# First attention: the transfers of the maximum rows issued by ACT instead of SyncE

## The reference: what is computed

```python
qkv = (x @ Wqkv).reshape(B, T, 3, H, D).transpose(2, 0, 3, 1, 4)    # 16 heads of 8
q, k, v = rope(qkv[0]), rope(qkv[1]), qkv[2]
att = einsum('bhqd,bhkd->bhqk', q, k) * scale
att = softmax(where(causal, att, -inf), axis=-1)
out = einsum('bhqk,bhkd->bhqd', att, v).transpose(0, 2, 1, 3).reshape(B, T, C)
x = layernorm(x + out @ Wo + bo)
```

## Time and profile before

| | |
|---|---|
| median of 3 runs | 1115.69 us (1115.14 to 1118.65) |
| profiled execution | 1117.81 us, of which 1116.1 us are the span from the first to the last instruction |
| busy: PE, DVE, ACT, POOL | 65%, 56%, 48%, 44% of the span |
| exps of the first attention, L2370 | 96 of 1023 ns |
| reduces of the first attention, L2319 and L2322 | 96 of 1223 ns |
| transfers of a load, L2136 | 192, median 0.68 to 0.69 us to issue |
| transfers of maximum rows, L2144 | 64 of 6 KB, median 0.70 us to issue |

### The profile page before, as it was taken

How to read it: one execution, slowest core, us unless ns; L and a number is a source line. 1 busy time by engine, 2 the same in 40 slices (tenths; PEclk the granted TensorE clock), 3 DMA queues, 4 the chain that set the end, 5 groups by cost and what they waited for, 6 DMA issues and landing times. The chain is left out here.

```text
span 1116.1 us, 20000 instructions
## 1 busy us (share of the span) xinstructions
PE 727.9 (65%) x6532; PEld 411.1 (37%) x6532; DVE 624.4 (56%) x1502; ACT 530.7 (48%) x849; POOL 491.0 (44%) x594
## 2 busy tenths in 40 slices
PE   3822578888847899999768499999681112386700
PEld 1411244444423344444233256556370111254500
DVE  2943468677556877777766223233477789321214
ACT  1420456666625666666457477777421006422102
POOL 0871346555542455555336444444208100468831
PEclk8965689999969999999989699999855555599955
DMA  7533322222000000000036899888006200144454
GB/s 156 177 118 90 108 67 69 66 73 71 6 1 1 0 1 1 1 1 1 1 113 213 204 186 181 150 155 155 2 0 193 75 1 1 27 89 91 60 116 124
DMA packets 138476, 87.72 MB, mean 79 GB/s; under 512 B 10722, under 2 KB 134050, under 8 KB 138274
## 3 DMA queue, kind: packets, MB, share of 16 engines
q1 hardware_dynamic: 132770, 82.57, 30.7%
q0 software_dynamic: 5632, 4.20, 2.8%
HBM read 56.99 MB, written 29.36 MB: 77 GB/s over the span
## 5 line engine op out<-in xcount | busy, mean ns | idle before, releaser
L1211 POOL TENSOR_TENSOR m_prod<-m_upc,m_gatec 128x512 f32<-128x512 f32 x64 | 99.6, 1557 | 114.7 <-DVE m_upc L1063 114.7
L2370 ACT ACTIVATE a_prob<-a_ps_pair 128x1024 f32<-128x1024 f32 x96 | 96.5, 1023 | 59.8 <-PE a_ps_pair L2181 56.8
L2411 POOL TENSOR_SCALAR_AFFINE_SELECT a_prob<-a_prob 128x512 f32<-128x512 f32 (+1 forms) x96 | 75.5, 787 | 105.7 <-ACT a_prob L2370 105.1
L2319 DVE TENSOR_REDUCE a_mx<-a_ps_pair 128x4 f32<-128x1024 f32 x64 | 78.0, 1223 | 77.6 <-PE a_ps_pair L2222 77.5
L751 POOL TENSOR_SCALAR_AFFINE_SELECT a_prob<-a_prob 128x512 f32<-128x512 f32 (+1 forms) x96 | 75.5, 787 | 97.3 <-ACT a_prob L713 97.3
L713 ACT ACTIVATE a_prob<-a_ps_b 128x1024 f32<-128x1024 f32 x96 | 98.6, 1029 | 31.2 <-PE a_ps_b L448 29.5
L1798 POOL DMA_INDIRECT m_y<-normed,m_idx x32 | 31.0, 970 | 103.2 <-DVE m_idx L1886 93.7
L1153 ACT ACTIVATE m_gate<-m_ps_g,bgu 128x512 f32<-128x512 f32 x64 | 43.9, 686 | 53.5 <-PE m_ps_g L914 53.4
L937 PE MATMUL m_ps_d<-m_act,wd 128*128 128x512 f32 x128 | 65.6, 594 | 2.3 <-DVE m_act L1073 2.3
L914 PE MATMUL m_ps_g<-m_x1T,wgu 128*128 128x512 f32 x128 | 65.8, 596 | 0.0
L916 PE MATMUL m_ps_u<-m_x1T,wgu 128*128 128x512 f32 x128 | 65.4, 592 | 0.0
(11 more groups left out here) (281 smaller groups left out, 1818.2 us busy)
## 6 DMA issues: line engine op xcount, KB each, us to landing
scratch_q<-p_parts SPq DMA_DIRECT2D x16, 384.0 KB, 2.6
scratch_k<-p_parts SPq DMA_DIRECT2D x16, 384.0 KB, 2.6
qst<-scratch_q SPq DMA_DIRECT2D x32, 192.0 KB, 3.3
kst<-scratch_k SPq DMA_DIRECT2D x32, 192.0 KB, 4.0
w<-in_w SPq DMA_DIRECT2D x8, 578.0 KB
qst<-scratch_q SPq DMA_DIRECT2D x64, 64.0 KB, 3.5
kst<-scratch_k SPq DMA_DIRECT2D x64, 64.0 KB, 4.0
qst<-scratch_q SPq DMA_DIRECT2D x32, 128.0 KB, 3.4
```

What stands on the lines that cost most here:

```text
L1211: nc.gpsimd.tensor_tensor(prod[:, n % 2, :], upc[:, n % 2, :], gatec[:, n % 2, :], ALU.mult).then_inc(s_pr, 1)
L2319: nc.vector.reduce_max(mx[:, w % 2, :, 2 * f:2 * f + 2, 1:2], pair[p][:, :].rearrange("p (m h k) -> p m h k", m=2, h=2), AX_X).then_inc(s_ ...
L2370: nc.scalar.activation(prob[:, r % 6, :], pair[(0, 2, 1)[j]][:, :], ACT.Exp, scale=scale, bias=0.0).then_inc(s_e, 1)
L2411: nc.gpsimd.affine_select(out=blk, in_=blk, compare_op=ALU.is_ge, fill=0.0, base=0, pattern=[[0, n], [1, P]], channel_multiplier=-1).then_ ...
```

## The change

The two transfers of maximum rows of a slot move from SP's program to ACT's. They stand at the end of ACT's turn, behind `exp(u, 2)`, and wait for the same copy as before. `copy_max` gets a wait until the transfers that read the same place of `mT` two slots earlier have landed. SP keeps the loads and the later weights; its loop starts at u = 0.

```diff
-                def max_rows(w):
-                    sp.wait_ge(s_mTc, w + 1)
-                    for m in range(2):
-                        r0 = 64 * m + max_row
-                        sp.dma_start(qst[r0:r0 + 3, w % BUFS, :, :].rearrange("p h (x q) -> p (h x) q", q=P),
-                                     mT[24 * m:24 * m + 24, w % 2, :]).then_inc(s_mrow[w % 2], 16)
...
-                for u in range(1 - LEAD, NU):
-                    if u + 2 < NU:
-                        max_rows(u + 2)
-                    if u % 2 == 1 and 0 <= u and u + BUFS < NU:
+                for u in range(NU):
+                    if u % 2 == 1 and u + BUFS < NU:
                         load((u - 1 + BUFS) // 2)
...
                 def copy_max(w):
                     act.wait_ge(s_mT, w + 1)
+                    after(act, s_mrow[w % 2], 32 * (w // 2))
                     nc.scalar.activation(mT[:, w % 2, :], ps_y[0:48, 0:64].bitcast(BF16), ACT.Copy).then_inc(s_mTc, 1)
+
+                def max_rows(w):
+                    act.wait_ge(s_mTc, w + 1)
+                    for m in range(2):
+                        r0 = 64 * m + max_row
+                        act.dma_start(qst[r0:r0 + 3, w % BUFS, :, :].rearrange("p h (x q) -> p (h x) q", q=P),
+                                      mT[24 * m:24 * m + 24, w % 2, :]).then_inc(s_mrow[w % 2], 16)
...
                     if 0 <= u < NU:
                         exp(u, 2)
+                    if 0 <= u + 2 < NU:
+                        max_rows(u + 2)
```

## The result

The changed kernel takes 1080.34 us (median of 4 runs, 1078.48 to 1081.46) against 1117.17 for the kernel before, run beside it (1115.14 to 1120.32). The ratio is 0.9666, with a 95% interval of 0.9637 to 0.9696: 36.8 us less, where 38.2 were predicted. The profiled execution took 1080.62 us with a span of 1078.9. In the changed file the lines stand a little higher: L2171 is the first scores matmuls (L2181 before), L2195 the fill that needs the stacks (L2205), L2360 the exps (L2370), L2365 the copy of the maxima (L2374), and L2372 is the new issue on ACT. L2309 and L2312 are the reduces, L2242 the transposed maxima, L2412 the mask and L2420 to L2426 `split_max`, the four small steps in which POOL splits the maxima.

A forecast was written before the change was run, and what follows sets the result against it. SP's issuing of transfers was taken to bound the first attention; 24.0 us up to slot 6 plus 14.2 us after it, with ACT's share nothing, made 38.2 us less: 1077.5 us, range 1070 to 1100 (1070 to 1084 without rivals).

The forecast's parts named there:

- The start: First attention, slot 0: ACT issues the rows behind its copy; PE's wait of 24.06 us shrinks to 0.6, saving 23.4.
- Slots 0 to 5: First slots of the first attention: slot 6 starts at 135.0 us instead of 159.04, 24.0 us gained.
- The new wait: Slot 5: PE waits 4.1 us for the fifth load, which SP issues only behind the later weights.
- slot 5 8.00 - 2.34 = 5.66: Slot 5's duration, taken as its old 8.00 us without its old wait of 2.34.
- Slots 6 to 31: Rest of the first attention: of 15.5 us in ten waits for maximum rows, 14.2 us come back.
- some 6 us: First attention: estimated gain, only in the range's best case, if lower-clock spells behind some PE waits go too.
- ACT's share at nothing: ACT in the first attention: its 64 added issues cost nothing, since its sequencer runs ahead of its compute.
- the upper end: ACT held 0.755 us by each issue: 11.4 us for two slots, 1.2 above 10.2, costing 15 us.
- Rival 1: ACT issues in series with its compute, 11.4 us for two slots: 23 us gained, 1092 us; chance 0.20.
- Rival 2: Both queues share what generates transfers, so 11.94 us stays the period: some 16 us gained, 1100 us; chance 0.13.
- Rival 3: Slower: an issue holds ACT's compute 1.4 us or more; gain gone at 13.9 us a pair; chance 0.06.
- Rival 4: No change: rows are issued earlier but land no earlier, the rings being full of stack loads; 1116 us; chance 0.03.

The follow-up runs named there:

- sp_first4: The changed kernel, but SP issues the maximum rows of slots 0 to 3 and ACT those of 4 to 31; 1093.7 us.
- act_first4: The changed kernel, but ACT issues the maximum rows of slots 0 to 3 and SP those of 4 to 31; 1099.72 us.
- weights_last: The changed kernel, but SP issues the later weights behind its last load of a stack instead of ahead of the fifth; 1071.51 us.
- before_third_exp: The changed kernel, but ACT issues the two transfers ahead of the third exp of the turn instead of behind it; 1122.62 us.
- split_first: The changed kernel, but POOL splits the maxima of slot u + 2 ahead of the first mask of slot u; 1075.8 us.
- four_issues: The changed kernel, but each transfer is cut in two, so ACT issues four in a slot instead of two; 1113.88 us.

## Why the prediction was right, step by step

**The bound was read rightly.** SP's issuing set both parts, and sp_first4 and act_first4 give back one part each: slot 0 waits 24.09 us with SP issuing the first rows, and rounds take 11.9 us with SP issuing the later ones.

**The start.** Predicted: 23.4 us saved, the reduce late next. Measured from the first fill, slot 0 begins at 12.70 us instead of 36.00: 23.3.

**Slots 0 to 5.** Here the sum was too good by 3.5 us. I had slot 6 49.3 us after the first fill (135.0 - 85.74); it came at 52.8. The new wait was named in its place and nearly in its size, 4.91 against 4.1: the fifth load's issue began 1.0 us later behind the first fill than I had put it and took 5.39 + 4.50 us, not 8.92, while slot 5 began 1.3 us later than forecast. The step that failed is "slot 5 8.00 - 2.34 = 5.66": taking the old duration without its wait leaves out what a wait does to the clock behind it. Without the wait the slot lasted 7.15, where weights_last, which has no wait there, takes 5.81. Slot 4's rows cost 0.68 and slots 1 to 3 some 0.5 more, which I had not counted: the rows' 1.2 us to land were taken from rows where the DMA engines were nearly idle, and were 5.75 here.

**Slots 6 to 31.** Here it was too low by 4.5. From slot 6 to slot 30 the kernel before took 142.68 us and the changed one 123.95, 18.7 less against the 14.2 of the sum. The term that was mis-sized is the lower clock: I had left its return out of the sum and put it in the range as "some 6 us". By subtraction it is about 5: without its 15.5 us of waits the old part is 127.2, and twelve pairs at 10.20 make 122.4. The trace of before shows where it lies. Of the twelve pairs seven take 10.2 us without their waits, all at a granted clock of 1.00. Four, which begin with slots 6, 12, 18 and 26, take 12.3, 11.4, 11.2 and 11.3 us at 0.75, 0.86, 0.86 and 0.85; together they are 5.3 us over 10.2 each (the last pair is 0.5 under). Two neighbours, columns as in the earlier trace rows:

```profile
220.24:232.36 12.12, 9.54 (x188) 5.70 (x188) 8.98 (x13) 7.67 (x11) 6.69 (x16) 1.00 0.25 70
232.36:244.25 11.89, 10.93 (x188) 6.28 (x189) 7.95 (x9) 7.67 (x11) 6.42 (x16) 0.86 0.25 70
```

The same 188 matmuls keep PE busy 1.4 us longer, and without the wait at its end (1.92 and 0.70) the first pair takes 10.20 us and the second 11.19. In the changed kernel the stretch from 140 to 260 us has no such pair. So the 18.7 us are 15.5 of waits and 4.8 of clock, less 1.6 by which the new pairs are longer than 10.20. before_third_exp shows the reverse, clock lost behind each wait.

**ACT's share at nothing** was nearly right. Two slots take 10.36 us, 0.16 above the 10.2 I had used, 1.9 over twelve pairs; the upper end was 15. The way was not quite the predicted one: the issue doesn't only overlap, it holds back the following exp until it is done, and it is the exp ahead that hides it. I had asked only when PE needs the delayed exp; POOL's mask needs it too, and the split of the maxima stands behind the mask. With split_first the same issue costs PE nothing that shows.

**The errors cancel, which is luck:** -3.5 and +4.5 in the stage, and +2.3 and -4.3 outside it that belong to no step. The total, 2.8 us off the median, is better than its parts; 1.5 of the 2.8 are the kernel before, whose median had moved from 1115.69 to 1117.17.

**The rivals.** Rival 1 (ACT serial, 11.4 us for two slots) is excluded in this place by 10.36, and before_third_exp shows that it is only the place that excludes it. Rival 2 (a shared generator) is excluded as I had priced it: ACT's 1.50 at 191.94 lies wholly inside SP's 4.36 at 191.58, and SP's twelve loads take 9.01 us from first to last (186.93 to 195.94) against 8.92. Its sign, an issue of over 1 us, does appear, but for SP's loads in the kernel before as well (at most 1.47 us there and 1.61 after, median 0.68 in both). The Trainium skill ("Perfetto Trace Analysis", DMA Instruction — HWDGE) has a generator locked for exclusive use; a lock as long as an issue is not borne out between ACT and SP, a shorter one inside it these rows can't exclude. Rival 3 set the break at 13.9 us for two slots; before_third_exp took 13.7 and came out 0.5% slower. With the 20.5 us that the first slots really gained (slot 6 began 73.3 us after the first fill before and 52.8 after) instead of 24.0 the break is 11.9 + 20.5 / 12 = 13.6, and it fits. Rival 4 fell with the first scores at 96.15.

**The Trainium skill's other rule** ("Advanced Engine Details and Errata", Sequencer and Instruction Queues) holds in part. An exp ahead of the transfer in the program runs beside its issue; the one behind it starts only 0.10 us after the issue, in the changed kernel and in four_issues alike.

## What to carry to other kernels

In these profiles an engine shows no busy time for the transfers it issues, so add up the durations of its issues over one period and hold the sum against the period: here 11.94 of 12.02 us was the whole story, and an in-order list of transfers that nobody needs yet was the rest. Here the moved issues were nearly free on ACT where they stood just behind an instruction about as long as they are, or in a pause of ACT; 1.5 us in the wrong place, one call earlier, turned 3.3% of gain into 0.5% of loss. Issue small urgent transfers early enough to survive another queue's bulk traffic, and when one wait goes, look at the next in-order queue (here SP's weights and POOL's mask, together worth another 1.2%).

## What the runs showed of the hardware

An issue on ACT (0.73 us, median of the small transfers; SP needed 0.70 for the same) blocks ACT's later compute for its whole length, but not the instruction ahead. It didn't lengthen with SP issuing beside it, except for the first pair of all, 2.15 us, whose cause stays open.

A small transfer took 1.2 us from the end of issue to PE's start where the DMA engines were 10% and 3% busy between the two (120.51 to 121.74 and 219.06 to 220.24 in the kernel before), and 4.4, 4.7, 5.6 and 5.75 us in the four cases above, where weights kept them 92%, 87%, 93% and 100% busy, though it was issued on a queue of its own.

A wait of PE of 1.4 us was enough to bring matmuls at the lower clock behind it (before_third_exp), so that such waits cost more than their length: 4.91 us cost 6.25. Which of them do it stays open: the 2.83 us in the earlier trace rows is followed by 0.39 for four matmuls, the 2.34 by 0.61.
